# Weight sums of a Strassen-type query projection made in the context stage, and one raw slot for each weight block

## What is computed

```
def _L0_xattn_ref(latents, context, Wq, Wk, Wv, Wo):
    hidden_states = jnp.concatenate([context, latents], axis=1)
    q = (latents @ Wq).reshape(b, q_len, N_KV_HEADS, N_GROUPS, HEAD_DIM)
    k = (hidden_states @ Wk).reshape(b, kv_len, N_KV_HEADS, HEAD_DIM)
    v = (hidden_states @ Wv).reshape(b, kv_len, N_KV_HEADS, HEAD_DIM)
    scores = jnp.einsum('bqhgd,bkhd->bhgqk', q, k) * scale
    attn = jax.nn.softmax(scores.astype(jnp.float32), axis=-1)
    out = jnp.einsum('bhgqk,bkhd->bqhgd', attn, v)
    return out.reshape(b, q_len, N_HEADS * HEAD_DIM) @ Wo
...
x = x + _L0_xattn_ref(_layernorm(x), ctx_4096, Wq, Wk, Wv, Wo)
x = x + _L0_ffn_ref(_layernorm(x), ...)
```

## Time and profile before

| | us |
|---|---|
| median of 3 runs | 1933.01 (1930.24 to 1934.89) |
| the profiled execution | 1931.98 |
| its span, first to last instruction | 1930.1 |
| PE busy | 1819.9 |
| DVE, ACT, POOL busy | 756.1, 644.5, 751.1 |
| moved by DMA | 225.8 MB, 117 GB/s on average |

### The profile page before, as it was taken

One profiled execution on the slowest core, in us unless ns is written; L12 is line 12 of the kernel. 1 busy time (PEld: TensorE's weight loads), 2 busy tenths in 40 slices (PEclk: granted clock), 3 DMA queues, 4 the chain that ended last, 5 costly groups with the idle time before them and its releaser, 6 DMA issues.

```text
span 1930.1 us, 27285 instructions
## 1 busy us (share of the span) xinstructions
PE 1819.9 (94%) x9254; PEld 1633.2 (85%) x9254; DVE 756.1 (39%) x1239; ACT 644.5 (33%) x1256; POOL 751.1 (39%) x539
## 2 busy tenths in 40 slices
PE   8999999977777778999999999999999999999997
PEld 7989888876676777998999899899888888888886
DVE  3511124533332335761474167327615432212216
ACT  3222122322222225761474167227623212212321
POOL 2121300555554555562355245415446422222242
PEclk9999999998888889999999999999999999999998
DMA  8435322233334334441253224314325321111134
GB/s 283 162 125 177 113 107 87 80 120 120 120 120 149 130 120 169 158 141 64 82 160 123 83 86 154 105 62 135 119 99 186 110 98 55 55 54 55 54 99 163
DMA packets 108976, 225.80 MB, mean 117 GB/s; under 512 B 14976, under 2 KB 73344, under 8 KB 108032
## 3 DMA queue, kind: packets, MB, share of 16 engines
q1 hardware_dynamic: 108928, 225.14, 35.1%
HBM read 156.21 MB, written 68.91 MB: 117 GB/s over the span
## 4 chain that ended last, share of the span: by engine, by line
PE 49%; issue 30%; POOL 16%; ACT 1%; DVE 1%; DMA 1%; POOLq 1%; ACTq 0%; SPq 0%; DVEq 0%
PE bank L1334 16%; PE bank L1336 16%; PE bank L1335 16%; POOL tile_region L675 6%; POOL tile_region L652 3%; POOL small_region L655 2%; POOL slab_split L655 2%; POOL slab_split L622 2%; PE bank L1527 1%; POOL act_region L655 1%; PE bank L1364 1%; ACT slab_split L809 0%; DMA q_scratch<-y_region 0%; ACT slab_split L717 0%; PE bank L1393 0%
## 5 line engine op out<-in xcount | busy, mean ns | idle before, releaser
L1334 PE MATMUL bank<-act_region,slab_split 128*128 128x512 f32 (+2 forms) x992 | 373.6, 377 | 80.2 <-DVE tile_region L1158 78.5
L622 POOL TENSOR_TENSOR slab_split<-slab_raw,slab_split 128x1024 fp32r<-128x1024 f32 x94 | 225.0, 2394 | 463.6 <-ACT slab_split L717 463.6
L1335 PE MATMUL bank<-act_region,slab_split 128*128 128x512 f32 (+2 forms) x992 | 370.7, 374 | 0.0
L1336 PE MATMUL bank<-act_region,slab_split 128*128 128x512 f32 (+2 forms) x992 | 370.3, 373 | 0.0
L675 POOL TENSOR_TENSOR tile_region<-tile_region,small 128x487 f32<-128x487 f32 x224 | 216.1, 1001 | 208.5 <-DVE small L1106 208.5
L1334 PEld LDWEIGHTS bank<-act_region,slab_split 128*128 128x128 f32 x992 | 193.3, 195 | 107.5 <-issue 80.5
L717 ACT ACTIVATE slab_split<-slab_raw 128x1024 fp32r<-128x1024 f32 x94 | 99.4, 1057 | 378.7 <-PE bank L1336 378.6
L1335 PEld LDWEIGHTS bank<-act_region,slab_split 128*128 128x128 f32 x992 | 193.6, 195 | 20.5
L1336 PEld LDWEIGHTS bank<-act_region,slab_split 128*128 128x128 f32 x992 | 193.3, 195 | 20.5
L1143 DVE TENSOR_TENSOR y_region<-y_region,bank 128x512 f32 (+2 forms) x96 | 59.5, 620 | 365.6 <-PE bank L1336 365.6
L1334 PE MATMUL bank<-mid_region 128*128 128x488 f32 (+2 forms) x480 | 198.9, 414 | 2.4 <-DMA mid_region<-k_latents_scratch 1.9
(11 more groups left out here) (151 smaller groups left out, 2996.2 us busy)
## 6 DMA issues: line engine op xcount, KB each, us to landing
slab_raw<-in_slabs SPq DMA_DIRECT2D x126, 512.0 KB, 3.5
q_scratch<-y_region SPq DMA_DIRECT2D x16, 1792.0 KB, 7.6
mid_region<-q_scratch SPq DMA_DIRECT2D x32, 896.0 KB, 5.7
v_scratch<-slab_split SPq DMA_DIRECT2D x8, 1536.0 KB, 6.6
mid_region<-v_scratch SPq DMA_DIRECT2D x32, 384.0 KB, 3.2
k_ctx_scratch<-small_region SPq DMA_DIRECT2D x32, 375.0 KB, 3.9
mid_region<-k_ctx_scratch SPq DMA_DIRECT2D x32, 375.0 KB, 5.7
tile_region<-in_ctxT SPq DMA_DIRECT2D x7, 1500.0 KB, 10.1
```

What stands on the lines that cost most here:

```text
L622: pool.tensor_tensor(WS[s][1], RAWS[s], f32(WS[s][0]), ALU.subtract).then_inc(s_wlo, 1)
L1334: pe.matmul(out_ap, w[0], a[0], start=first, stop=False)
L1335: pe.matmul(out_ap, w[0], a[1], start=False, stop=False)
L1336: return pe.matmul(out_ap, w[1], a[0], start=False, stop=last)
```

## The change

**The sums move.** In each context batch b SP now also loads the raw slabs of pairs 2b and 2b+1, one pair at a time into `slab_raw`; POOL makes the four sums in place (`weight_sums`), and SP stores `slab_raw` (1.05 MB) into the DRAM array `weight_sums_scratch`. A load waits for the store before it, a store for the sums. POOL's own order is: sums of the even pair, `ctx_lo` of the next batch, sums of the odd pair.

**The blocks load singly.** In the query stage each of the seven blocks has a raw slot (`WRAW`, 0.26 MB), loaded from the slabs or from the scratch array when POOL has read that block of the pair before. POOL has only the seven low parts left. The slots take the place of `SRAW`, so three of the four combined quarters now share one buffer `CT` and wait for its last reader.

```
+            def store_sums(j):
+                sp.wait_ge(s_sum, 4 * (j + 1))
+                sp.dma_start(s_d[j], RAW[:, :]).then_inc(s_sst, 16)
+
+            def store_ctx(b, first=False):
                 for u in range(NKV):
                     sp.wait_ge(s_ev, N_CTX * b + u + 1)
                     sp.dma_start(kc_d[u, b], f32(KST[u % 2][:, :, 0:SC])).then_inc(s_kst[u % 2], 16)
+                    if u == 0:
+                        if not first:
+                            sp.wait_ge(s_sst, 32 * b)
+                        load_pair(2 * b)
+                    if u == 2:
+                        store_sums(2 * b)
+                    if u == 3:
+                        sp.wait_ge(s_sst, 32 * b + 16)
+                        load_pair(2 * b + 1)
+                sp.wait_ge(s_ev, N_CTX * b + N_CTX - 1)
+                store_sums(2 * b + 1)
                 sp.wait_ge(s_ev, N_CTX * b + N_CTX)
                 sp.dma_start(v_d[:, b, :, 0:6 * D].rearrange("h p c -> p h c"),
...
+            def next_blocks(j):
+                for n in range(N_Q):
+                    sp.wait_ge(s_blo, N_Q * j + n + 1)
+                    load_block(j + 1, n)
...
-            store_pair(0)
-            for j in range(1, PAIRS):
-                if j < PAIRS - 1:
-                    sp.wait_ge(s_blo, N_Q * j + N_Q - 1)
-                    load_pair(j + 1)
-                else:
+            for j in range(PAIRS):
+                if j < PAIRS - 2:
+                    next_blocks(j + 1)
+                if j == PAIRS - 1:
...
+            def weight_sums(j):
+                pool.wait_ge(s_rawq, 32 * (j + 1))
+                W11, W12, W21, W22 = [part(RAW, i * 512, 512) for i in range(4)]
+                for n, (out, a, b, op) in enumerate([(W22, W21, W22, ALU.add), (W21, W11, W21, ALU.subtract),
+                                                     (W11, W22, W11, ALU.subtract), (W12, W12, W11, ALU.subtract)]):
+                    if n:
+                        pool.wait_ge(s_sum, 4 * j + n)
+                    pool.tensor_tensor(out, a, b, op).then_inc(s_sum, 1)
+
             ctx_lo(1, 1)
-            with pool.Fori(1, B // 2) as i:
+            weight_sums(0)
+            weight_sums(1)
+            with pool.Fori(0, B // 2 - 1) as i:
                 for j in range(2):
-                    ctx_lo(2 * i + j, j)
+                    weight_sums(4 * i + 2 * j + 2)
+                    ctx_lo(2 * i + j + 2, j)
+                    weight_sums(4 * i + 2 * j + 3)
...
             def block_hi(j, n):
-                if BLOCKS[n][0] == "S":
-                    act.wait_ge(s_sum, 4 * (j + 1))
-                else:
-                    act.wait_ge(s_rawq, 32 * (j + 1))
-                act.activation(WB[n][0], WSRC[n], ACT.Copy).then_inc(s_bhi, 1)
+                act.wait_ge(s_wr[n], 16 * (j + 1))
+                act.activation(WB[n][0], WRAW[n], ACT.Copy).then_inc(s_bhi, 1)
...
-                combine(2, 4, C22, U3, GB[3], ALU.add)
+                combine(2, 4, CT, U3, GB[3], ALU.add)
...
+                dve.wait_ge(s_qlo, FREE + 4 * j + 1)
+                combine(5, 6, CT, U3, GB[1], ALU.subtract)
...
+                dve.wait_ge(s_qlo, FREE + 4 * j + 3)
+                combine(6, 7, CT, U2, GB[2], ALU.add)
```

More of the change, by code:

```diff
@@ L229, in xattn_ffn @@
         WB += [[part(RA, l * XT_AT + 2 * NK * HALF, 512) for l in range(2)]]
[L230 to L234, removed]
+        WRAW = [part(RAW, i * 512, 512) for i in range(4)] + [part(FB, i * 512, 512) for i in range(3)]
+        SUMS = {"S2": 0, "S4": 1, "S3": 2, "S1": 3}
+        P1C, U3 = [part(FB, at, HALF) for at in (3500, 2500)]
+        U2, CT = [part(YR, 8 * ROWS + i * HALF, HALF) for i in range(2)]
         PRAW = [RAWS[0], RAWS[1], part(FB, 3 * PIECE, PIECE)]
@@ L294, in xattn_ffn @@
         s_rawq = sem("query_slabs_loaded")
+        s_sst = sem("weight_sums_stored")
+        s_wr = sems("weight_block_loaded", 7)
         s_sum = sem("weight_sums")
@@ L458, in store_ctx, with load_block @@
                              f32(part(RC, 0, 6 * NKV * D)).rearrange("p (h c) -> p h c", h=NKV)).then_inc(s_vst, 16)
+            def load_block(j, n):
+                name = BLOCKS[n]
+                if name[0] == "S":
+                    block = s_d[j, :, SUMS[name] * 512:(SUMS[name] + 1) * 512]
+                else:
+                    block = slabs[T_Q + 2 * j + int(name[1]) - 1, :, (int(name[2]) - 1) * 512:int(name[2]) * 512]
+                sp.dma_start(WRAW[n], block).then_inc(s_wr[n], 16)
+            def next_blocks(j):
+                for n in range(N_Q):
+                    sp.wait_ge(s_blo, N_Q * j + n + 1)
+                    load_block(j + 1, n)
             def next_ctx(b):
@@ L462, in next_ctx @@
                 sp.dma_start(CRAW, ctxT[b + 1]).then_inc(s_ctx, 16)
-            store_ctx(0)
+            store_ctx(0, True)
             with sp.Fori(1, B - 1) as b:
@@ L475, in _ @@
                     n += 1
+                    if n == C_LAT + 2:
+                        sp.wait_ge(s_sst, 16 * PAIRS)
+                        sp.wait_ge(s_clo, B - 1)
+                        for i in range(N_Q):
+                            load_block(0, i)
                 if g[0] == "vl":
@@ L636, in ctx_lo @@
                 pool.tensor_tensor(HT[j][:, 1, :, 0:SC], CRAW, f32(HT[j][:, 0, :, 0:SC]), ALU.subtract).then_inc(s_clo, 1)
+            def weight_sums(j):
[6 more added lines that the diff above has]
+                    pool.tensor_tensor(out, a, b, op).then_inc(s_sum, 1)
             ctx_lo(1, 1)
[L639 removed]
+            weight_sums(0)
+            weight_sums(1)
+            with pool.Fori(0, B // 2 - 1) as i:
                 for j in range(2):
[L641 to L652 removed]
+                    weight_sums(4 * i + 2 * j + 2)
+                    ctx_lo(2 * i + j + 2, j)
+                    weight_sums(4 * i + 2 * j + 3)
+            weight_sums(PAIRS - 2)
+            weight_sums(PAIRS - 1)
+            def weight_blocks_lo(j):
                 for n in range(N_Q):
                     pool.wait_ge(s_bhi, N_Q * j + n + 1)
[L655 to L657 removed]
+                    pool.tensor_tensor(WB[n][1], WRAW[n], f32(WB[n][0]), ALU.subtract).then_inc(s_blo, 1)
             weight_blocks_lo(0)
@@ L661, in _ @@
             with pool.Fori(1, PAIRS) as j:
-                pool.wait_ge(s_blo, N_Q * j)
                 weight_blocks_lo(j)
             pool.wait_ge(s_blo, N_Q * PAIRS)
-            pool.memset(part(FB, 0, QT * PP).rearrange("p (i c) -> p i c", i=QT)[:, 0:4, KEYS:PP], 0.0).then_inc(s_pad, 1)
+            pads = part(FB, 0, QT * PP).rearrange("p (i c) -> p i c", i=QT)[:, :, KEYS:PP]
+            pool.memset(pads[:, 0:5, :], 0.0).then_inc(s_pad, 1)
             pool.wait_ge(s_q, N_Q * PAIRS - 4)
@@ L668, in _ @@
             pool.wait_ge(s_comb, FREE + N_COMB * PAIRS - 1)
-            pool.wait_ge(s_qlo, FREE + 4 * PAIRS - 2)
-            pool.memset(part(FB, 0, QT * PP).rearrange("p (i c) -> p i c", i=QT)[:, 4:QT, KEYS:PP], 0.0).then_inc(s_pad, 1)
+            pool.memset(pads[:, 5:QT, :], 0.0).then_inc(s_pad, 1)
             def p_normalise(n):
```

30 lines of the change are left out of this document (8 added, 22 removed).

## The result

The changed kernel takes 1877.02 us (median of 4 runs, 1873.67 to 1879.37) against 1933.25 for the kernel before on the same chip (4 runs, 1930.24 to 1934.89). The ratio is 0.971, 95% interval [0.969, 0.9729]: 56 us faster, where 63 were forecast. The profiled execution has a span of 1875.8 us, 54.3 less than before.

What follows compares the result with a forecast made beforehand. It took a query-stage ring of slab transfer, sums and splitting, 24.7 us a pair, to hold PE. 112.3 us saved there, 49 lost in the context stage: -63 against 1932.0, so 1870 us; forecast's own range 1855 to 1893.

Steps and rivals of the forecast that it cites:

- Bound and query stage: Query stage: transfer, sums and splitting take 24.7 us a pair; after the change PE bounds it at 17.0, saving 112.3.
- (a): Query stage: POOL's seven low parts are 9 to 12 us of work in a pair's 17.
- (b): Query stage: waits of two combinations for shared buffer CT add nothing; a tenth of a microsecond each would be hidden.
- (c): Query stage: 0.26 MB loads overlap in the queue, 10.3 us a pair for 3.7 MB, against 24.7 if none overlap.
- Rival 2: Query stage becomes bound by its small loads: a pair at 20 us, 45 us more, 1915 us; chance 0.08.
- the 1891 worked out from the Trainium skill: Query stage: at 138 GB/s, seven loads and a store take 18.4 us a pair, 1.4 over PE: 1870 + 21.
- Start: Context stage: first loads, sums and stores delay context 2, landing at 76.7; low part 98.0, batch 2 21.4 us late.
- Ring: Context stage: chained loads, sums and stores through one raw copy take 38.1 us a batch, 4.8 over PE's 33.3.
- load of the odd pair 5.2: Context stage: the odd pair's raw slab load, with its second issue, takes 5.2 us of each 38.1 us batch.
- End of the stage: Last context batch: late K tile store holds ACT and a layer norm's bank, 1 to 2 us; cold restart 2 us.
- Rival 1: Context stage: the chain of transfers and sums fits under PE at 33.4 us, only the start's loss stays: 1845; chance 0.10.
- Rivals 3 and 4: 3: scratch traffic halves context-stage DMA rate, 1954, chance 0.04; 4: query-stage wait moves to another DVE combination, 1930, chance 0.03.

## Why the prediction was right, and where it was off

**Bound and query stage: right.** The ring of one raw copy, its transfer and its sums held PE; PE's pace is 84 matmuls at 0.2027 us, 17.02 us against 17.0, and the stage gave 111.9 us against 112.3. The kernel without the ring shows it by itself (111 us). Points (a) and (b), that POOL's low parts and the shared buffer CT cost nothing, hold, since no wait is left. Point (c), that loads of 0.26 MB overlap in the queue, was the open one: with twice as many and 5.5 MB a pair PE waited once. Rival 2's 1915 did not come, nor did the 1891 worked out from the Trainium skill. The 138 GB/s of its "DMA: Bandwidth & Descriptors", Bandwidth, is for transfers of 64 KB issued from GpSimd; no run here has one, and the blocks of 256 KB, issued by SP, moved with the pair's store at 216 GB/s, which is what PE's pace asked for (3.7 MB in 17.04 us), and with the extra copies at 325. The same page's Rules for kernel authors asks for 1 MiB or more where the most bandwidth is wanted; this stage did not need that much, and its loads are issued well ahead of PE's need, so that PE waited for none.

**Start: right.** Context 2 was split at 76.06 (forecast 76.7), the low part ended at 98.69 (98.0), 22.1 us late (21.4). Moving that one load ahead of the store gave 8.3 of them back.

**Ring: right in kind, 1.1 us short.** Forecast 38.1, measured 39.2, the mean of five. Step by step, also as means of the five, from S, the end of an odd pair's sums: the context landed at S + 13.8 (forecast 13.7; the batch shown above, with 14.8, is the odd one out), the even pair at S + 17.8 (17.7); the two sets of sums took 5.4 each (5.1), the store 4.3 (5.0) and the odd pair's load 6.3 (5.2). So the queued transfers were right, and the term that failed is "load of the odd pair 5.2", 1.1 us short; the store's 0.7 too much hid more than half of it, which is luck. A K tile's store of 0.38 MB stands between the two (172.95 above) and is in no term of the forecast. It landed 5.7 us after its issue, at 178.7, 2.2 us into the odd pair's load, and at the forecast's 0.36 MB/us its bytes are 1.1 us; that it made the load longer was not tested. In all 29.2 us were lost in five rings where 24 were counted.

**End of the stage: a second term short.** "In the last batch a K tile's late store holds up ACT and by it a layer norm's bank (1 to 2 us)", with 2 us for a cold restart: 3 to 4 were counted and 6.7 measured. The mechanism is the one named: ACT waits 9.56 us at 315.90 for the K store, and PE for the layer norm before 317.64. Set beside the same matmuls of the kernel before, that wait is 3.4 us, and the lower clock behind it 1.6. Another 1.4 is the lower clock behind the ring's last wait, at 294.68. So there were two cold restarts where one was counted, and the wait was twice its term. In the kernel with the low part first this same path carried 21.2 us.

In all 57.9 us late against 49, and the query stage as forecast: 54.3 between the two spans against 63, 56 between the medians. The range's own terms add up to 1860 to 1899, not to the 1855 to 1893 that was written; the result lies in both. Rival 1, a ring at PE's 33.3 us, needed 0.43 MB/us for the queued transfers and 1 us less for store and load each. The store did come out 0.7 us shorter, but the load 1.1 longer, and the queued 4.2 MB took 13.8 us, where 0.43 gives 4.2 / 0.43 + 2.05 = 11.8. Rivals 3 and 4 are excluded by the ring of 39.2 us and by PE's gapless query stage.

## What to carry to other kernels

Work that is moved under an idle engine still has its place in a queue: count the ring that it closes (load, sums, store through one buffer) against the pace of the engine that it is hidden behind, and with it every transfer that stands between two uses of that buffer. Where such a ring is a few microseconds too long, halve the buffer and let the halves overlap, and keep loads that the critical path needs ahead of stores that wait. A load in pieces that an engine can start on one by one, ahead of a large store, can release a stage without being issued any earlier. When an edit removes one wait and the time stays, look for the same lag at another buffer.

## What was not expected of the hardware

- With the DMA engines busy all the time at 325 GB/s (the kernel with the extra copies) PE's matmuls started 0.2067 us apart with a granted clock of 1.00, against 0.2027 at 216 GB/s in the changed kernel: 2% slower without any wait, in all 13 periods. It ended with the query stage (1186.3 us from the first score matmul to the end, as ever). Its cause was not tested.
- A store of 1.05 MB held the raw copy 4.1 us and one of 0.07 MB 1.9, each with a K tile's store issued 0.6 us behind it: by these two a fixed part of 1.7 us and 0.44 MB/us, where the store and load of the earlier trace rows together gave 0.36.
- Four sums in a chain, each waiting for POOL's own last result, start 1.36 us apart and take 5.40 us, against 5.1 for four of the same size with two such waits; 0.08 us of each step lies between the two instructions.
